# GpSimd adds each scan state's contribution to y_acc, and VectorE writes state times C to a buffer of its own

## The chip, the cores and the metric

The kernel runs on one core of one Trainium2 chip. The metric is the device time of one execution in microseconds. Of the five engines, TensorE does the matmuls and transposes, VectorE (DVE in the rows) and ScalarE (ACT) the elementwise work, SyncE (SP) issues all DMAs, and GpSimd (POOL) has no part in the kernel before. Each engine runs its own list of instructions in order, and they meet through semaphores.

## The reference, cut to what matters

x is 1024 tokens (16 sequences of 64) by 512. Three blocks follow each other, each with a residual.

```
x = x + cross_attention(layernorm(x), ctx)          # 8 heads, 512 keys for each sequence
n = layernorm(x)                                    # selective scan:
u = silu(conv4(n @ Wx) + cb)                        # 1024 channels, 4 taps
delta = softplus(n @ Wdt + b);  B, C = n @ Wb, n @ Wc   # 16 states
for t in time, for s in 16 states:
    h[s] = exp(delta * A[s]) * h[s] + delta * u * B[s]
    y   += C[s] * h[s]                              # starts from D * u
x = x + y @ Wout
x = x + sum over the top 4 of 16 experts (gate, up, down) of layernorm(x)
```

The line that matters is the one with C[s]: y is a sum over 16 states.

## The kernel before, in words

The tokens are cut into G = 4 groups of 256 (four sequences). A tile of one group's 1024 channels is 128 partitions x 2048 (8 blocks of channels by 256 tokens), f32. A state of the scan is four operations of VectorE over such tiles, in `scan_step`: part 0 writes u times B to `state` (L1074), part 1 runs the recurrence over time in place (L1077, `tensor_tensor_scan` with `decay`), part 2 multiplies `state` by C in place (L1080), part 3 adds it into `y_acc` (L1084). ScalarE makes `decay` for two states ahead (`scan_decay`, L855; two buffers), SyncE loads the broadcast rows of B and C (`load_bc`, L361; two buffers `bc_bcast`). ScalarE starts `y_acc` with D times u (`y_start`, L841), and TensorE reads the finished `y_acc` in the output projection (`out_proj`, L602, for the last group L674), after `step_done` has counted all states of the group.

The order on each engine is written out by hand. Groups overlap: while group g scans, the attention of group g + 1 runs. For VectorE the group loop reads: states 0 to 3 (LEAD = 4, with `key_bias`, L1017, after state 1), then 8 attention units with one state each, the unit's `neg_max` (L1023) between parts 0 and 1 and its `invert_sums` (L1065) between parts 1 and 2; then states 12 and 13 (TAIL = 2), `add_tiles` (L1031, the attention's result into `x_tokens`), the norm, and the signal `x1_rdy` on which SyncE loads the projection weights. States 14 and 15 follow while TensorE projects, then the convolution (`conv`, L1043), `scan_inputs`, and state 0 of the next group. In the next group's first state part 3 stands after `add_tiles` of the group before it.

The last group's states 1 to 15 run beside the experts: 64 jobs, in each of which TensorE does gate and up (`split_matmul`, L634) and down (L665). Jobs 4 to 42 hold the 60 parts of these states, one or two in each job (`scan_parts`). Beside them VectorE subtracts the high half of a weight to get the low half (`split_lo`, L1161), multiplies the gated pair (`hidden`, L1167 and L1168, PSUM inputs) and adds an expert's output into `x_tokens` (`add_expert`, L1179, PSUM input).

The convolution reads `conv_in`, whose three pad columns in front of each sequence VectorE zeroes once at the start (L1196).

Of the kernel before, what the change touches and what calls it, by code (L numbers as in the profile page):

```python
# [20 lines left out]
ALU = mybir.AluOpType  # L21
# [8 lines left out]
T = 64  # L30
# [4 lines left out]
G = 4  # L35
# [94 lines left out]
def perceiver_block(nc, x, ctx_t, ctx_n, wq_t, wk, wv_t, xp_t, dt_t, bc_t, ow_t, gate_t,  # L130
                    eg_t, eu_t, ed_t, params, bc_dram, out):
    with ExitStack() as es:
# [3 lines left out]
        def sem(name):  # L136
            return es.enter_context(nc.semaphore(name))
# [8 lines left out]
        comb_ = sb("comb", G * NT * E)  # L146
# [6 lines left out]
        hs_ = sb("state", SW)  # L153
        acc_ = sb("y_acc", SW)
# [10 lines left out]
        lgs = [sb(f"route_logits_{c}", NT * E)[:, :] for c in range(G)]  # L165
        sc, sfc, gs = (sb(f"route_{n}", NT * E)[:, :] for n in ("score", "choice", "group"))
# [11 lines left out]
        with ExitStack() as early:  # L178
# [13 lines left out]
            xi_ = sb("conv_in", 2 * 2 * XP, stack=early)  # L192
            xi = [xi_[:, s * 2 * XP:(s + 1) * 2 * XP].rearrange("p (k t) -> p k t", t=T + TAPS - 1) for s in range(2)]
# [37 lines left out]
        rank_ = sb("rank_scratch", 2 * NT * E * E)  # L231
        rk1, rk2 = (rank_[:, k * NT * E * E:(k + 1) * NT * E * E] for k in range(2))
# [58 lines left out]
        scan_rd = sem("decay_read")  # L291
        step_done = sem("scan_step_done")
# [38 lines left out]
        def _(sp):  # L331
# [24 lines left out]
            def load_bc(k):  # L356

                if k >= 2:
                    sp.wait_ge(step_done, k - 1)
                src = bc_dram[k // NS].rearrange("(w s) t -> s w t", w=2)[k % NS]  # L360
                sp.dma_start(bcs[k % 2], src.unsqueeze(0).to_broadcast([P, 2, GT])).then_inc(bc_in[k % 2], 16)  # L361
# [344 lines left out]
        def _(act):  # L706
# [98 lines left out]
            def proj_x(g, k0):  # L805
                n = g * NBK // 2 + k0 // 2
                b = job_a()
                act.wait_ge(pad_rdy, 1)
# [161 lines left out]

        @block.vector
        def _(dve):
# [60 lines left out]

            def conv(g, k0):
# [32 lines left out]
            def scan_step(g, j, parts=range(SCAN_PARTS)):  # L1067
# [11 lines left out]
                if 2 in parts:  # L1079
                    step(dve.tensor_tensor(h3, h3, cs, ALU.mult))  # L1080
                if 3 in parts:
                    if j == 0:
                        dve.wait_ge(ys_rdy, g + 1)
                    dve.tensor_tensor(acc_[:, :], acc_[:, :], h, ALU.add).then_inc(step_done, 1)  # L1084
                    dve.wait_ge(step_done, n + 1)
# [109 lines left out]
            for s in range(2):  # L1195
                ins = dve.memset(xi[s][:, :, 0:TAPS - 1], 0.0)  # L1196
            ins.then_inc(pad_rdy, 1)
# [15 lines left out]
            add_tiles(0)  # L1213
            dve.nop().then_inc(x1_rdy, 1)
# [7 lines left out]
            for g in range(G - 1):  # L1222
# [14 lines left out]
                add_tiles(g + 1)  # L1237
                dve.nop().then_inc(x1_rdy, 1)
# [96 lines left out]
```

## Time and profile before

| | us |
|---|---|
| Three runs | 1514.64, 1515.77, 1516.62 |
| Median | 1515.77 |
| Profiled execution, span from first to last instruction | 1514.9 |
| TensorE busy | 1281.5 |
| VectorE busy | 1157.1 |
| ScalarE busy | 599.0 |
| GpSimd busy | 0.2 |

The profiled execution has no time of its own beside its span; the runs' median lies 0.9 us above the span. Busy time is the sum of an engine's instruction times. An engine that is busy most of the time in a stretch may set its length; the chain of work that ended last, followed back from the end, says which engine did. The slices below cut the span in 40 parts of 37.9 us; a digit is a busy share in tenths.

```profile
PE   6998578868859758858758898999999999998998
DVE 1201899998999998999998848979888888446554
ACT  4432754554655535745536611131313131022220
POOL 0000000000000000000000000000000000000000
```

### The profile page before, as it was taken

What the parts mean: (1) busy time and instruction counts of PE and PEld (TensorE: products, weight loads), DVE (VectorE), ACT (ScalarE), POOL (GpSimd) and SP (SyncE); (2) the same over time, 40 slices, a digit from 0 to 9 for tenths busy, and PEclk for the clock granted to TensorE, in tenths of its full rate; (3) what the DMA queues carried; (4) which work ended last, traced back from release to release, by engine and by line L of the source; (5) the groups of instructions that cost most, each with busy time, mean ns of one, the idle gap of its engine ahead of it and who ended that gap; (6) DMA issues with size and microseconds to landing.
All of it is one profiled execution on the core that took longest, in us unless ns stands there. A gap on an engine that the chain in (4) does not pass through costs nothing.

```text
span 1514.9 us, 16115 instructions
## 1 busy us (share of the span) xinstructions
PE 1281.5 (85%) x6400; PEld 965.9 (64%) x6400; DVE 1157.1 (76%) x1001; ACT 599.0 (40%) x1229; POOL 0.2 (0%) x4
## 2 busy tenths in 40 slices
PE   6998578868859758858758898999999999998998
PEld 4776446646536547536537586777777777676775
DVE  1201899998999998999998848979888888446554
ACT  4432754554655535745536611131313131022220
POOL 0000000000000000000000000000000000000000
PEclk9999878988978978979879789999999999999999
DMA  7333013324013324013314201222222312114553
GB/s 247 101 121 127 6 25 116 104 63 133 8 49 91 118 54 128 10 49 110 89 57 145 91 22 35 86 61 70 56 77 63 84 49 63 56 44 152 168 160 103
DMA packets 95930, 128.47 MB, mean 85 GB/s; under 512 B 4976, under 2 KB 70640, under 8 KB 95856
## 3 DMA queue, kind: packets, MB, share of 16 engines
q1 hardware_dynamic: 95856, 127.45, 27.9%
q8 instruction: 51, 0.84, 0.2%
q14 instruction: 23, 0.19, 0.0%
HBM read 125.21 MB, written 2.23 MB: 84 GB/s over the span
## 4 chain that ended last, share of the span: by engine, by line
DVE 55%; PE 31%; ACT 8%; issue 3%; DMA 2%; DVEq 0%; ACTq 0%; SPq 0%
DVE state L1077 16%; PE bank L634 11%; DVE y_acc L1084 8%; DVE state L1074 8%; DVE state L1080 7%; PE bank L591 6%; PE bank L665 6%; ACT decay L855 4%; DVE x_tokens L1179 3%; DVE w_lo L1161 2%; DMA queries_ctx<-in_dt_t 2%; PE bank L520 2%; PE bank L545 2%; DVE hidden L1168 2%; DVE hidden L1167 2%
## 5 line engine op out<-in xcount | busy, mean ns | idle before, releaser
L1077 DVE TENSOR_TENSOR_SCAN state<-decay,state 128x2048 f32<-128x2048 f32 x64 | 282.9, 4420 | 8.3 <-ACT decay L855 7.2
L665 PE MATMUL bank<-w_down,hidden 128*128 128x512 f32 x512 | 232.1, 596 | 5.2 <-DVE x_tokens L1179 5.2
L634 PE MATMUL bank<-x_hi,w_hi 128*128 128x256 f32 x1024 | 192.6, 312 | 12.2 <-DVE hidden L1168 7.5
L855 ACT ACTIVATE decay<-delta_odd,params 128x256 f32<-128x256 f32 x256 | 106.3, 498 | 197.7 <-DVE state L1077 186.8
L634 PEld LDWEIGHTS bank<-x_hi,w_hi 128*128 128x128 f32 x1024 | 150.3, 198 | 43.5 <-issue 30.4
L520 PE MATMUL bank<-ctx,queries_ctx 128*128 128x256 f32 x512 | 151.8, 449 | 22.2 <-ACT queries_ctx L748 22.2
L634 PE MATMUL bank<-x_hi,w_lo 128*128 128x256 f32 x1024 | 168.9, 288 | 0.0
L634 PE MATMUL bank<-x_lo,w_hi 128*128 128x256 f32 x1024 | 168.7, 288 | 0.0
L902 ACT ACTIVATE hidden<-bank 128x512 f32<-128x512 f32 x64 | 38.0, 594 | 327.6 <-PE bank L665 321.5
L665 PEld LDWEIGHTS bank<-w_down,hidden 128*128 128x128 f32 x512 | 93.3, 191 | 100.5 <-issue 94.2
L1084 DVE TENSOR_TENSOR y_acc<-y_acc,state 128x2048 f32<-128x2048 f32 x64 | 146.7, 2292 | 2.3
L1080 DVE TENSOR_TENSOR state<-state,bc_bcast 128x2048 f32<-128x2048 f32 x64 | 146.2, 2284 | 1.4
L1167 DVE SCALAR_TENSOR_TENSOR hidden<-hidden,bank 128x512 f32<-128x512 f32 x64 | 43.8, 685 | 135.0 <-ACT hidden L902 134.8
L634 PEld LDWEIGHTS bank<-x_hi,w_lo 128*128 128x128 f32 x1024 | 145.6, 198 | 0.0
L634 PEld LDWEIGHTS bank<-x_lo,w_hi 128*128 128x128 f32 x1024 | 145.6, 197 | 0.0
L545 PE MATMUL bank<-probs,ctx 128*128 128x256 f32 x512 | 132.7, 417 | 14.9 <-ACT probs L782 14.9
L520 PEld LDWEIGHTS bank<-ctx,queries_ctx 128*128 128x128 f32 x512 | 109.1, 224 | 53.5 <-ACT queries_ctx L748 23.8
L855 ACT ACTIVATE decay<-delta_even,params 128x256 f32<-128x256 f32 x256 | 107.0, 500 | 79.7 <-DVE state L1077 71.3
L545 PEld LDWEIGHTS bank<-probs,ctx 128*128 128x128 f32 x512 | 104.4, 209 | 40.6 <-ACT probs L782 17.1
L591 PE MATMUL bank<-normed_t,queries_ctx 128*128 128x256 f32 x512 | 112.3, 381 | 2.4 <-DMA queries_ctx<-in_dt_t 1.3
L591 PEld LDWEIGHTS bank<-normed_t,queries_ctx 128*128 128x128 f32 x512 | 96.8, 190 | 19.5 <-DMA queries_ctx<-in_dt_t 3.7
L1161 DVE TENSOR_TENSOR w_lo<-raw_w,w_hi 128x1024 fp32r<-128x1024 f32 x64 | 77.0, 1224 | 33.3 <-ACT w_hi L883 31.9
(128 smaller groups left out, 1328.1 us busy)
## 6 DMA issues: line engine op xcount, KB each, us to landing
ctx<-in_ctx_t SPq DMA_DIRECT2D x32, 512.0 KB, 6.3
ctx<-in_ctx_n SPq DMA_DIRECT2D x32, 512.0 KB, 3.5
bc_bcast<-bc_scratch SPq DMA_DIRECT2D x64, 256.0 KB, 5.1
raw_w<-in_eg_t SPq DMA_DIRECT2D x32, 512.0 KB, 4.3
raw_w<-in_eu_t SPq DMA_DIRECT2D x32, 512.0 KB, 4.0
w_down<-in_ed_t SPq DMA_DIRECT2D x32, 512.0 KB, 4.8
queries_ctx<-in_dt_t SPq DMA_DIRECT2D x4, 2048.0 KB, 10.0
queries_ctx<-in_xp_t SPq DMA_DIRECT2D x4, 2048.0 KB, 14.8
```

What stands on the lines that cost most here:

```text
L520: pe.matmul(o, QT[:, k, c, qb * P:(qb + 1) * P], ctxT[n % 2][:, c, :], start=(c == 0), stop=False)
L545: mm = pe.matmul(b[:, cc * Q:(cc + 1) * Q], ctxN[n % 2][:, j, c * P:(c + 1) * P], probT[n % 2][:, j, :], start=(j == 0), stop=(j == KC - 1))
L591: mm = pe.matmul(b[:, kk * GT:(kk + 1) * GT], w[:, c, (k + kk) * P:(k + kk + 1) * P], xT[:, c, :], start=(c == 0), stop=(c == DC - 1))
L634: mm = pe.matmul(o, w[a](k), x[b](k), start=(q == 0), stop=(q == len(terms) - 1))
L665: mm = pe.matmul(b[t][:, :], hid[j % 2][:, i * GT + t * P:i * GT + (t + 1) * P], w_dn[k % 2][:, i, :], start=(i == 0), stop=(i == IC - 1))
L855: ins = act.activation(dA[n % 2][:, k * GT:(k + 1) * GT], dlt[g % 2][:, k, :], ACT.Exp, scale=par[:, c:c + 1])
L1074: step(dve.tensor_tensor(h3, u[g % 2], bs, ALU.mult))
L1077: dve.tensor_tensor_scan(h, dA[n % 2], h, 0.0, ALU.mult, ALU.add).then_inc(scan_rd, 1)
L1080: step(dve.tensor_tensor(h3, h3, cs, ALU.mult))
L1084: dve.tensor_tensor(acc_[:, :], acc_[:, :], h, ALU.add).then_inc(step_done, 1)
L1161: dve.tensor_tensor(lo, raw[q % RAW], hi, ALU.subtract).then_inc(w_rdy, 1)
L1167: step(dve.scalar_tensor_tensor(out=o, in0=o, scalar=1.0, in1=b[0][:, :], op0=ALU.add, op1=ALU.mult))
```

## The change

Part 3 leaves VectorE. Part 2 no longer multiplies in place: it writes to a new tile `state_c` and counts it in `hc_rdy`. GpSimd runs a list of its own: for each of the 64 states it waits for `hc_rdy`, adds `state_c` into `y_acc` and counts `step_done`. There is one `state_c`, so part 2 of the next state waits for `step_done` of the last one. SyncE's load of the next B and C rows waits for `hc_rdy` where it waited for `step_done`. To make room for the 8 KB a partition of `state_c`, `conv_in` moves into the memory of `probs`, where the attention overwrites its pads, so VectorE zeroes them once per group (`conv_pads`), and the small tiles of the router move behind the buffers of the experts.

```diff
+        hc_ = sb("state_c", SW)
...
-            xi_ = sb("conv_in", 2 * 2 * XP, stack=early)
-            xi = [xi_[:, s * 2 * XP:(s + 1) * 2 * XP].rearrange("p (k t) -> p k t", t=T + TAPS - 1) for s in range(2)]
+            xi = [pp_[:, s * 2 * XP:(s + 1) * 2 * XP].rearrange("p (k t) -> p k t", t=T + TAPS - 1) for s in range(2)]
...
                 if k >= 2:
-                    sp.wait_ge(step_done, k - 1)
+                    sp.wait_ge(hc_rdy, k - 1)
...
-                act.wait_ge(pad_rdy, 1)
+                act.wait_ge(pad_rdy, g + 1)
...
+        @block.gpsimd
+        def _(pool):
+            for n in range(G * NS):
+                if n % NS == 0:
+                    pool.wait_ge(ys_rdy, n // NS + 1)
+                pool.wait_ge(hc_rdy, n + 1)
+                pool.tensor_tensor(acc_[:, :], acc_[:, :], hc_[:, :], ALU.add).then_inc(step_done, 1)
+                pool.wait_ge(step_done, n + 1)
...
+            def conv_pads():
+                for s in range(2):
+                    ins = dve.memset(xi[s][:, :, 0:TAPS - 1], 0.0)
+                ins.then_inc(pad_rdy, 1)
...
                 if 2 in parts:
-                    step(dve.tensor_tensor(h3, h3, cs, ALU.mult))
-                if 3 in parts:
-                    if j == 0:
-                        dve.wait_ge(ys_rdy, g + 1)
-                    dve.tensor_tensor(acc_[:, :], acc_[:, :], h, ALU.add).then_inc(step_done, 1)
-                    dve.wait_ge(step_done, n + 1)
+                    if n >= 1:
+                        dve.wait_ge(step_done, n)
+                    dve.tensor_tensor(hc_[:, :].rearrange("p (k t) -> p k t", k=NBK), h3, cs, ALU.mult).then_inc(hc_rdy, 1)
+                    dve.wait_ge(hc_rdy, n + 1)
...
-            for s in range(2):
-                ins = dve.memset(xi[s][:, :, 0:TAPS - 1], 0.0)
-            ins.then_inc(pad_rdy, 1)
...
             add_tiles(0)
+            conv_pads()
             dve.nop().then_inc(x1_rdy, 1)
...
                 add_tiles(g + 1)
+                conv_pads()
                 dve.nop().then_inc(x1_rdy, 1)
```

VectorE in an attention unit of the first group's scan, before; `state_c_ready` below is the semaphore `hc_rdy`, `scan_step_done` is `step_done`.

```order
L1074 TENSOR_TENSOR state<-u_even,bc_bcast 128x2048 [waits bc_in1,scan_step_done]
L1023 TENSOR_REDUCE neg_max<-bank 128x2 [waits scores_full,dve_step]
L1077 SCALAR_TENSOR_TENSOR state<-decay,state 128x2048 [waits decay_ready]
L1065 RECIPROCAL row_sum<-row_sum 128x2 [waits probs_exp,decay_read]
L1080 TENSOR_TENSOR state<-state,bc_bcast 128x2048
L1084 TENSOR_TENSOR y_acc<-y_acc,state 128x2048 [waits dve_step]
L1074 TENSOR_TENSOR state<-u_even,bc_bcast 128x2048 [waits bc_in0,scan_step_done]
```

The same unit on VectorE with the change.

```order
L1090 TENSOR_TENSOR state<-u_even,bc_bcast 128x2048 [waits bc_in1,state_c_ready]
L1034 TENSOR_REDUCE neg_max<-bank 128x2 [waits scores_full,dve_step]
L1093 SCALAR_TENSOR_TENSOR state<-decay,state 128x2048 [waits decay_ready]
L1081 RECIPROCAL row_sum<-row_sum 128x2 [waits probs_exp,decay_read]
L1098 TENSOR_TENSOR state_c<-state,bc_bcast 128x2048 [waits scan_step_done]
L1090 TENSOR_TENSOR state<-u_even,bc_bcast 128x2048 [waits bc_in0,state_c_ready]
```

The add is gone from the unit, and the product with C has a wait that it did not have.

VectorE where the last state before the projections (state 13) ends and the norm begins, before.

```order
L1084 TENSOR_TENSOR y_acc<-y_acc,state 128x2048 [waits dve_step]
L1031 TENSOR_TENSOR x_tokens<-x_tokens,bank 128x512 [waits bankD_full,scan_step_done]
L1031 TENSOR_TENSOR x_tokens<-x_tokens,bank 128x512 [waits bankD_full]
L989 BN_STATS stats<-x_tokens 128x6 [waits bankD_free]
L989 BN_STATS stats<-x_tokens 128x6 [waits dve_step]
```

The same place with the change.

```order
L1098 TENSOR_TENSOR state_c<-state,bc_bcast 128x2048 [waits scan_step_done,decay_read]
L1042 TENSOR_TENSOR x_tokens<-x_tokens,bank 128x512 [waits bankD_full,state_c_ready]
L1042 TENSOR_TENSOR x_tokens<-x_tokens,bank 128x512 [waits bankD_full]
L1047 MEMSET probs 128x8x3 [waits bankD_free]
L1047 MEMSET probs 128x8x3
L1000 BN_STATS stats<-x_tokens 128x6
```

Here the add is gone too, and the two pad memsets stand ahead of the norm.

GpSimd's list with the change, its start; before, it held four memsets and nothing else.

```order
L972 UNCONDITIONAL_BRANCH [waits barrier_Pool_Activation_PE_DVE_SP_gather]
L978 ISA
L978 TENSOR_TENSOR y_acc<-y_acc,state_c 128x2048 [waits state_c_ready,y_started]
L978 TENSOR_TENSOR y_acc<-y_acc,state_c 128x2048 [waits state_c_ready,scan_step_done] x15
L978 TENSOR_TENSOR y_acc<-y_acc,state_c 128x2048 [waits state_c_ready,y_started,scan_step_done]
```

All 64 adds stand there, each behind its own product with C and the add ahead of it.

## Rows read from the trace of the kernel before

**Rows 1.** The page, part 1: busy time, share of the span, instructions.

```profile
PE 1281.5 (85%) x6400; PEld 965.9 (64%) x6400; DVE 1157.1 (76%) x1001; ACT 599.0 (40%) x1229; POOL 0.2 (0%) x4
```

**Rows 2.** The page, part 4: the chain that ended last, by engine.

```profile
DVE 55%; PE 31%; ACT 8%; issue 3%; DMA 2%; DVEq 0%; ACTq 0%; SPq 0%
```

**Rows 3.** The view by stretches, all engines; the columns stand in its first line.

```profile
core 0: us, PE busy (x) PEld busy (x) DVE busy (x) ACT busy (x) POOL busy (x), PEclk, DMA share, GB/s
397.65:564.45 166.80, 121.87 (x503) 86.07 (x501) 164.74 (x75) 88.87 (x217) 0.00 (x0) 0.85 0.25 71
564.45:616.33 51.88, 43.78 (x170) 32.24 (x171) 45.04 (x48) 26.58 (x42) 0.00 (x0) 0.86 0.32 97
868.00:1240.00 372.00, 358.17 (x2141) 283.75 (x2140) 295.74 (x321) 91.44 (x175) 0.00 (x0) 0.98 0.21 59
948.00:1240.00 292.00, 286.77 (x1734) 225.90 (x1733) 245.15 (x193) 76.64 (x148) 0.00 (x0) 0.99 0.24 67
```

**Rows 4.** VectorE in order of time, one attention unit of group 1.

```profile
444.81 2.29 DVE L1074 TENSOR_TENSOR state<-u_odd,bc_bcast 128x2048 f32<-128x2048 f32 x1
...
447.13 0.69 DVE L1023 TENSOR_REDUCE neg_max<-bank 128x2 f32<-128x512 f32 x1
...
447.74 4.41 DVE L1077 TENSOR_TENSOR_SCAN state<-decay,state 128x2048 f32<-128x2048 f32 x1
...
452.27 2.27 DVE L1080 TENSOR_TENSOR state<-state,bc_bcast 128x2048 f32<-128x2048 f32 x1
...
454.58 2.29 DVE L1084 TENSOR_TENSOR y_acc<-y_acc,state 128x2048 f32<-128x2048 f32 x1
...
456.90 2.29 DVE L1074 TENSOR_TENSOR state<-u_odd,bc_bcast 128x2048 f32<-128x2048 f32 x1
```

**Rows 5.** Groups of VectorE; columns: shapes, count, busy us, mean ns, idle before.

```profile
L1077 DVE TENSOR_TENSOR_SCAN state<-decay,state 128x2048 f32<-128x2048 f32 x64 | 282.9, 4420 | 8.3 <-ACT decay L855 7.2
...
L1084 DVE TENSOR_TENSOR y_acc<-y_acc,state 128x2048 f32<-128x2048 f32 x64 | 146.7, 2292 | 2.3
...
L1161 DVE TENSOR_TENSOR w_lo<-raw_w,w_hi 128x1024 fp32r<-128x1024 f32 x64 | 77.0, 1224 | 33.3 <-ACT w_hi L883 31.9
...
L1017 DVE TENSOR_TENSOR normed<-bank,params 8x2048 f32<-8x2048 f32 x4 | 9.1, 2279 | 15.9 <-PE bank L489 15.8
...
L1031 DVE TENSOR_TENSOR x_tokens<-x_tokens,bank 128x512 f32<-128x512 f32 x14 | 9.0, 683 | 18.1 <-PE bank L574 17.9
...
L1196 DVE MEMSET conv_in<- 128x24 f32 x2 | 0.1, 78 | 0.0
```

**Rows 6.** The same view of GpSimd, one of its four groups.

```profile
L1324 POOL MEMSET const-float32-0.0<- 128x1 f32 x1 | 0.1, 99 | 0.2 <-issue 0.2
```

**Rows 7.** The chain in order of time (start us, us, what): decay, then scan.

```profile
394.24 3.31 ACT decay L855 x8
397.65 4.44 DVE state L1077
```

**Rows 8.** VectorE in order of time, where group 1 hands over to group 2.

```profile
570.22 2.29 DVE L1074 TENSOR_TENSOR state<-u_odd,bc_bcast 128x2048 f32<-128x2048 f32 x1
...
585.22 4.42 DVE L1077 TENSOR_TENSOR_SCAN state<-decay,state 128x2048 f32<-128x2048 f32 x1 [1.27 <-ACT decay L855]
...
595.10 2.71 DVE L1043 SCALAR_TENSOR_TENSOR u_even<-conv_in,params,u_even 128x256 f32<-128x256 f32 x6 [0.80 <-ACT u_even L815]
...
600.17 5.34 DVE L1043 SCALAR_TENSOR_TENSOR u_even<-conv_in,params,u_even 128x256 f32<-128x256 f32 x12 [2.35 <-ACT u_even L815]
```

**Rows 9.** The same chain, one job of the expert stage: gate and up, then down.

```profile
1251.12 5.75 PE bank L634 x48
1256.87 3.44 PE bank L665 x8
```

**Rows 10.** The same chain: where two attention units of the first group begin.

```profile
52.12 3.65 PE bank L545 x16
...
61.11 3.65 PE bank L545 x16
```

More of the change, by code:

```diff
@@ L145, in perceiver_block @@
         bcT = nrm_[0:2 * NS, 0:GT]
-        comb_ = sb("comb", G * NT * E)
         xT_ = sb("normed_t", DC * GT)
@@ L163, in perceiver_block @@
         ident = par[:, C_ID:C_ID + P]
-        lgs = [sb(f"route_logits_{c}", NT * E)[:, :] for c in range(G)]
-        sc, sfc, gs = (sb(f"route_{n}", NT * E)[:, :] for n in ("score", "choice", "group"))
         st_ = sb("stats", 6 * G * NT)
@@ L231, in perceiver_block @@
         rank_ = sb("rank_scratch", 2 * NT * E * E)
+        comb_ = sb("comb", G * NT * E)
+        lgs = [sb(f"route_logits_{c}", NT * E)[:, :] for c in range(G)]
+        sc, sfc, gs = (sb(f"route_{n}", NT * E)[:, :] for n in ("score", "choice", "group"))
         rk1, rk2 = (rank_[:, k * NT * E * E:(k + 1) * NT * E * E] for k in range(2))
@@ L291, in perceiver_block @@
         scan_rd = sem("decay_read")
+        hc_rdy = sem("state_c_ready")
         step_done = sem("scan_step_done")
```

## The prediction, made before the changed kernel had run

> **What bounds the kernel now.** I read the busy times first: VectorE works 1157.1 us of the span of 1514.9, TensorE 1281.5, GpSimd 0.2 [rows 1]. The chain that ended last gives VectorE 55% of the span and TensorE 31% [rows 2]. Which of the two it is changes by stage, so the stretches come next [rows 3]. While the 14 scan states of group 1 run beside the attention of group 2 (397.65 to 564.45), VectorE is busy 164.74 of 166.80 us: it alone sets that stretch. There are three such stretches, for groups 0, 1 and 2. Between them (564.45 to 616.33) the chain goes through norm, weight transfer, projections and convolution; VectorE is busy 45.04 of 51.88 us there and runs states 14 and 15 while it would wait. In the expert stage (868 to 1240) TensorE is busy 358.17 of 372 us. So the 16 states of group 3 hardly touch the end: only the three VectorE stretches count.
>
> One attention unit of such a stretch [rows 4]: product with B at 444.81, neg_max at 447.13, scan at 447.74, product with C at 452.27, the add into y_acc at 454.58, the next product at 456.90. A unit is 456.90 - 444.81 = 12.09 us, and the add's slot in it 456.90 - 454.58 = 2.32 us (2.29 busy).
>
> **What is removed.** 64 adds of 2.29 us on VectorE [rows 5]. In each of the three stretches 14 of them (states 0 to 13) stand on the path: 14 x 2.32 = 32.5 us, 97.4 us in all. Those of states 14 and 15 and of group 3 are cover, worth nothing.
>
> **What is added.** 64 adds on GpSimd over the same 128x2048 tiles. The trace of before has no such operation: GpSimd did four memsets. From below I bound it by VectorE's own add, 2.29 us, from above by the slowest row over two tiles of this size, the scan of 4.42 us [rows 5]. GpSimd's memset of one element a partition takes 99 ns [rows 6], VectorE's of 24 takes 78 [rows 5]; of the two ends that is nearer to the slow one, and I take 4.42. The Trainium skill (GPSIMD Engine Reference, section "Elementwise — side-by-side cycle accounting") measures 4497 ns for this add against 2293 ns on VectorE; the trace agrees with the second, and by the first the sum below would be some 3 us higher.
>
> At 4.42 us the add is far shorter than a state, so if the two engines ran freely beside each other GpSimd would always be done before VectorE's next product with C, which now waits for it (one state_c buffer). The question is whether they run freely. Every VectorE operation of a state reads two tiles of SBUF, and so does the add. I forecast that the engines take turns: while GpSimd adds, no VectorE instruction with two SBUF inputs runs, and one waits for the other to end. Operations that read PSUM or a single tile go on. No row of before can show this, GpSimd being idle; it is a judgement, and the first rival is its opposite. The Trainium skill states it (SBUF — State Buffer, section "Who interferes with whom"): the second VectorE port pair is GpSimd's only one and "it's an exclusive lock"; no run here shows it yet. By that rule the change loses, without it it wins.
>
> **The sum with turns.** VectorE starts its next product about 0.03 us after the last (447.13 - 447.10 [rows 4]), and GpSimd, as an engine that is released by another, some 0.10 us after its releaser: the decay row ends at 394.24 + 3.31 = 397.55 and the scan that waited starts at 397.65 [rows 7]. So VectorE gets the next product with B in first, GpSimd takes its turn when that ends, and the scan follows. An add then costs 4.42 + 0.10 + 0.10 - 0.03 = 4.59 us of turn and returns 2.32: net 2.27 us, less what may run beside it. Per stretch:
> - Adds of states 3 to 10 fall beside a neg_max, which reads PSUM and takes 447.74 - 447.13 = 0.61 us of the path [rows 4]: 8 x (2.27 - 0.61) = 13.3 us.
> - Adds of states 2, 11 and 12 have nothing beside them: 3 x 2.27 = 6.8 us.
> - The add of state 1 falls beside the key-bias product from PSUM (2.28 us, the L1017 row [rows 5]): 0.
> - The add of state 0 falls beside two x_tokens adds from PSUM (2 x 0.68 = 1.3 us less overlap, the L1031 row [rows 5]): 1.0 us. Group 0 has no such adds, so 1.3 us more, once.
> - The add of state 13 falls beside x_tokens and the norm, which read PSUM or a single tile from 564.45 until the product at 570.22 [rows 8], over 4.6 us: the 2.3 us come off whole.
> That is 13.3 + 6.8 + 0 + 1.0 - 2.3 = 18.8 us; three stretches and the 1.3 make 57.7 us.
>
> States 14 and 15: the scan of 15 waited 1.27 us for its decay, the first convolution 0.80 us, the next ones 2.35 us [rows 8]. Two turns of 2.27 us go into these 4.4 us. I take 0; without that cover 4.5 us per hand-over.
>
> Expert stage: from 948 to 1240 VectorE is busy 245.15 of 292 us [rows 3], 47 us idle. A job of TensorE takes 5.75 + 3.44 = 9.19 us [rows 9], and 15 states are spread over 39 jobs, so a state has 39 x 9.19 / 15 = 23.9 us; 292 us hold 12.2 of them, with 3.9 us idle in each, and between a product with C and the next product with B a full set of PSUM-reading hidden and x_tokens operations always stands. Even bare, 2.27 us a state fits into 3.9. But an add that is under way blocks the w_lo subtraction (1.22 us, two SBUF inputs [rows 5]), and hidden and the down matmul queue behind that. I take 3 us for such moments, between 0 and 15 x 2.27 = 34.
>
> The pads: two memsets of 78 ns [rows 5] move from the start to each group, ahead of the signal that starts the weight load: 4 x 0.16, less 0.16 at the start, 0.5 us. ScalarE's wait for them is met long before, since norm, weight transfer and the first projections stand between. The B and C load on the sync queue now waits for the product with C, one add sooner than before, so it is never later. Where conv_in, comb and the logits lie in memory costs nothing, since attention of the group is over when conv_in is written.
>
> What queues behind the new waits: behind the product with C stands the whole VectorE queue, and through neg_max ScalarE's exponentials and TensorE's next scores; behind GpSimd's last add of a group stands only the output projection, which TensorE reaches only after the next group's projections.
>
> Sum: 57.7 + 0.5 + 3 = 61.2 us on the profiled span of 1514.9: 1576.1. The runs' median of 1515.77 lies 0.9 above that span; with it 1577 us.
>
> **The rivals.**
> 1. *The engines run freely (faster).* The 97.4 us come off, 0.5 us go on: 1515.8 - 96.9 = 1419 us. Would TensorE take over? A unit falls to 12.09 - 2.32 = 9.77 us, and the first group's attention, with no scan beside it, has units of 61.11 - 52.12 = 8.99 us [rows 10], so no. This decides if GpSimd's reads do not stop VectorE's. For it: no row shows a conflict. Against it: all it needs is the same tiles' memory at the same time.
> 2. *Turns, with no cover at all, or GpSimd served late.* If GpSimd's turn stops PSUM-reading work too, all 14 adds of a stretch cost 2.27: 3 x 31.8 = 95.3, with 0.5 and some 8 us in the expert stage 1620 us. If GpSimd only comes in after the scan, the neg_max cover alone is lost, 24 x 0.61 = 15 us: 1592.
> 3. *Turns, and the add as short as VectorE's.* 2.29 + 0.17 = 2.46 us a turn, 0.14 net. Per stretch 8 x (0.14 - 0.61) + 3 x 0.14 - 2.1 - 1.1 - 2.3 = -8.9; with the once-only 1.3 and 0.5 us, 1515.8 - 26.8 + 1.8 = 1491 us, faster. The point from which turns lose is an add of about 3.3 us. Against it: GpSimd's memset, slower than VectorE's.
> 4. *GpSimd falls behind its turn or its trigger, so that the wait for state_c does more than move the add.* It would need more than 9 us an add; I count it with rival 2.
>
> **Chances.** Forecast (turns, PSUM work beside them) 0.52, own range 1550 to 1600. Rival 2 0.26, rival 1 0.16, rival 3 0.04, and 0.02 for costs that cancel. What a measurement of this kernel can tell from no change is 0.2%, 3 us. Faster 0.20, same 0.02, slower 0.78. The range runs from 1486, a little under rival 3, to 1630, above rival 2, and leaves out the 0.16 of rival 1 and a little beyond the top.
>
> **What the changed profile would show.** Right: GpSimd adds end to start with VectorE's two-input operations; the unit's pitch near 12.09 + 1.66 = 13.75 us; an idle time of some 4 us in front of the scan in each unit while neg_max runs on time; expert stage as long as before; the stretch 397.65 to 564.45 longer by some 19 us. Wrong: a pitch of 9.8 us with GpSimd busy beside the scan (rival 1), neg_max late as well (rival 2), GpSimd adds starting well under 4 us apart in turn (rival 3), or a time under 1486.

## The result, and the profile after

| | before | after |
|---|---|---|
| Runs beside each other | 4 | 4 |
| Median, us | 1515.82 | 1550.29 |
| Lowest and highest, us | 1514.64 to 1516.62 | 1549.63 to 1552.22 |
| Span of the profiled execution, us | 1514.9 | 1548.9 |

The ratio after to before is 1.023, with an interval of 1.0215 to 1.0244: slower by 34 us. The forecast was 1577, slower by 61, with a range of 1486 to 1630; the result lies in the range, 27 us under the forecast and at the lower edge of the forecast's own 1550 to 1600. The page of after, part 1 and the head of part 4, to be read beside [rows 1] and [rows 2]:

```profile
PE 1287.7 (83%) x6400; PEld 968.2 (63%) x6400; DVE 1184.3 (76%) x943; ACT 596.7 (39%) x1229; POOL 372.4 (24%) x68
...
PE 48%; DVE 45%; ACT 5%; issue 2%; DMA 0%; DVEq 0%; SPq 0%; ACTq 0%
```

VectorE lost 64 adds of 2.29 us (146.7 us, [rows 5]) and its busy time rose all the same, from 1157.1 to 1184.3 us. GpSimd is busy 372.4 us. So something made VectorE's other operations longer. The groups of after, VectorE's and GpSimd's, say which (shapes, count, busy us, mean ns, idle before):

```profile
L1093 DVE TENSOR_TENSOR_SCAN state<-decay,state 128x2048 f32<-128x2048 f32 x64 | 414.1, 6470 | 15.3 <-ACT decay L856 14.1
L1098 DVE TENSOR_TENSOR state_c<-state,bc_bcast 128x2048 f32<-128x2048 f32 x64 | 146.2, 2284 | 1.4
...
L1090 DVE TENSOR_TENSOR state<-u_odd,bc_bcast 128x2048 f32<-128x2048 f32 x32 | 90.0, 2812 | 1.2
L1175 DVE TENSOR_TENSOR w_lo<-raw_w,w_hi 128x1024 fp32r<-128x1024 f32 x64 | 86.3, 1369 | 33.1 <-ACT w_hi L884 31.6
...
L1012 DVE TENSOR_SCALAR normed<-x_tokens,mean_var,rstd 128x512 f32<-128x512 f32 x16 | 10.0, 663 | 0.3
L1028 DVE TENSOR_TENSOR normed<-bank,params 8x2048 f32<-8x2048 f32 x4 | 9.1, 2279 | 15.5 <-PE bank L490 15.4
```

```profile
L978 POOL TENSOR_TENSOR y_acc<-y_acc,state_c 128x2048 f32<-128x2048 f32 x64 | 372.2, 5815 | 958.2 <-DVE state_c L1098 958.2
```

The scan's mean went from 4420 ns [rows 5] to 6470, w_lo's from 1224 to 1369; the product with C, which waits until GpSimd is done, kept its 2284, and the key-bias product from PSUM its 2279. In order of time the mechanism can be seen. VectorE and GpSimd in group 1 of after, around the adds of states 1 and 2 (433.52 and 447.12) and in one attention unit (from 473.67) (start us, us, engine, line), the counterpart of [rows 4]:

```profile
433.41 2.28 DVE L1028 TENSOR_TENSOR normed<-bank,params 8x2048 f32<-8x2048 f32 x1
435.83 4.35 DVE L1090 TENSOR_TENSOR state<-u_odd,bc_bcast 128x2048 f32<-128x2048 f32 x1
...
449.33 8.61 DVE L1093 TENSOR_TENSOR_SCAN state<-decay,state 128x2048 f32<-128x2048 f32 x1
...
473.67 2.29 DVE L1090 TENSOR_TENSOR state<-u_odd,bc_bcast 128x2048 f32<-128x2048 f32 x1
475.99 0.69 DVE L1034 TENSOR_REDUCE neg_max<-bank 128x2 f32<-128x512 f32 x1
476.60 8.00 DVE L1093 TENSOR_TENSOR_SCAN state<-decay,state 128x2048 f32<-128x2048 f32 x1
...
487.02 2.29 DVE L1090 TENSOR_TENSOR state<-u_odd,bc_bcast 128x2048 f32<-128x2048 f32 x1
```

```profile
433.52 4.52 POOL L978 TENSOR_TENSOR y_acc<-y_acc,state_c 128x2048 f32<-128x2048 f32 x1 [9.08 <-DVE state_c L1098]
447.12 6.54 POOL L978 TENSOR_TENSOR y_acc<-y_acc,state_c 128x2048 f32<-128x2048 f32 x1 [9.08 <-DVE state_c L1098]
...
473.78 6.54 POOL L978 TENSOR_TENSOR y_acc<-y_acc,state_c 128x2048 f32<-128x2048 f32 x1 [6.82 <-DVE state_c L1098]
```

One attention unit goes from the product with B at 473.67 to the next at 487.02: 13.35 us, where it was 12.09. GpSimd's row begins at 473.78, 0.11 us after VectorE's next product with B. That product takes its usual 2.29 us and ends at 475.96, neg_max from PSUM takes its usual 0.69, and the scan, which should take 4.42, takes 8.00. GpSimd's row ends at 480.32; 480.19 plus the scan's own 4.41 is where the scan ends. So the scan did its work only after the add (its last 0.13 us apart), and its waiting is inside its own duration: no idle time stands ahead of it. GpSimd's 6.54 us hold its own wait too: where it starts beside a PSUM product (433.52, key-bias) its row is 4.52 long. Beside the add of state 1 the next product with B takes 4.35 us for 2.29, and beside that of state 2, where nothing from PSUM stands, the scan 8.61 for 4.42. The two engines take turns, and each one's waiting for the other is printed as work.

The landmarks of both traces (each stretch is from the scan of state 0 to the first x_tokens addition behind state 13, each hand-over from there to the next group's scan of state 0), in us:

| | before | after | difference | forecast |
|---|---|---|---|---|
| start to the scan of state 0 of group 0 | 176.68 | 176.09 | -0.6 | |
| three stretches | 165.48, 166.80, 167.14 | 180.48, 180.82, 180.82 | +42.7 | +57.7 |
| three hand-overs | 55.49, 55.28, 63.59 | 56.42, 55.56, 66.05 | +3.7 | +0.5 |
| from the last group's scan of state 0 to the end | 664.44 | 652.66 | -11.8 | +3 |
| sum | 1514.9 | 1548.9 | +34.0 | +61.2 |

The stretches in the view by engine, after (the columns as in [rows 3]). The first is group 1's: VectorE is busy 179.24 of 180.82 us, as full as before. The third covers as much of the expert stage as the 868 to 1240 of before.

```profile
412.99:593.81 180.82, 126.05 (x503) 89.57 (x501) 179.24 (x60) 88.18 (x217) 81.08 (x13) 0.83 0.24 66
593.81:649.37 55.56, 47.23 (x178) 33.85 (x179) 46.87 (x48) 29.96 (x50) 15.61 (x3) 0.86 0.29 91
914.00:1286.00 372.00, 363.04 (x2195) 288.27 (x2195) 294.45 (x317) 91.29 (x175) 65.48 (x13) 0.98 0.21 62
```

In the same 372 us TensorE now gets through 2195 matmuls where it got through 2141 [rows 3]. A job is 56 of them and 9.19 us [rows 9], so after the 372 us it is 54 / 56 x 9.19 = 8.9 us further on (from 17.5 us behind the scan of state 0 to the end both traces hold the same 3613). The expert stage gained, where I had expected a small loss.

### The profile page after: what moved, and what is told of

It reads as the page before. It is cut to its first block, busy times and chain, and to the rows that moved or that the text cites. A ratio compares the mean times of both kernels' runs of the same rounds, so it can differ in the third digit from the quotient of the medians.

```text
span 1548.9 us, 16223 instructions
## 1 busy us (share of the span) xinstructions
PE 1287.7 (83%) x6400; PEld 968.2 (63%) x6400; DVE 1184.3 (76%) x943; ACT 596.7 (39%) x1229; POOL 372.4 (24%) x68
## 4 chain that ended last, share of the span: by engine, by line
PE 48%; DVE 45%; ACT 5%; issue 2%; DMA 0%; DVEq 0%; SPq 0%; ACTq 0%
DVE state L1093 21%; PE bank L635 20%; PE bank L666 12%; DVE state L1090 7%; DVE state_c L1098 6%; PE bank L592 6%; PE bank L521 2%; PE bank L546 2%; ACT decay L856 1%; DVE neg_max L1034 1%; PE bank L603 1%; PE bank L584 1%; PE bank L675 1%; DVE x_tokens L1193 1%; DVE w_lo L1175 1%
## 5 line engine op out<-in xcount | busy, mean ns | idle before, releaser
L978 POOL TENSOR_TENSOR y_acc<-y_acc,state_c 128x2048 f32<-128x2048 f32 x64 | 372.2, 5815 | 958.2 <-DVE state_c L1098 958.2
L1093 DVE TENSOR_TENSOR_SCAN state<-decay,state 128x2048 f32<-128x2048 f32 x64 | 414.1, 6470 | 15.3 <-ACT decay L856 14.1
L666 PE MATMUL bank<-w_down,hidden 128*128 128x512 f32 x512 | 232.1, 596 | 5.0 <-DVE x_tokens L1193 5.0
L521 PE MATMUL bank<-ctx,queries_ctx 128*128 128x256 f32 x512 | 156.3, 459 | 23.1 <-ACT queries_ctx L749 23.1
L666 PEld LDWEIGHTS bank<-w_down,hidden 128*128 128x128 f32 x512 | 93.3, 191 | 100.4 <-issue 94.2
L521 PEld LDWEIGHTS bank<-ctx,queries_ctx 128*128 128x128 f32 x512 | 112.6, 231 | 55.9 <-ACT queries_ctx L749 24.8
L1098 DVE TENSOR_TENSOR state_c<-state,bc_bcast 128x2048 f32<-128x2048 f32 x64 | 146.2, 2284 | 1.4
L1175 DVE TENSOR_TENSOR w_lo<-raw_w,w_hi 128x1024 fp32r<-128x1024 f32 x64 | 86.3, 1369 | 33.1 <-ACT w_hi L884 31.6
L592 PEld LDWEIGHTS bank<-normed_t,queries_ctx 128*128 128x128 f32 x512 | 98.3, 194 | 18.8 <-DMA queries_ctx<-in_dt_t 2.4
## 6 DMA issues: line engine op xcount, KB each, us to landing
queries_ctx<-in_xp_t SPq DMA_DIRECT2D x4, 2048.0 KB, 14.8
```

What stands on the lines that cost most here:

```text
L521: pe.matmul(o, QT[:, k, c, qb * P:(qb + 1) * P], ctxT[n % 2][:, c, :], start=(c == 0), stop=False)
L592: mm = pe.matmul(b[:, kk * GT:(kk + 1) * GT], w[:, c, (k + kk) * P:(k + kk + 1) * P], xT[:, c, :], start=(c == 0), stop=(c == DC - 1))
L666: mm = pe.matmul(b[t][:, :], hid[j % 2][:, i * GT + t * P:i * GT + (t + 1) * P], w_dn[k % 2][:, i, :], start=(i == 0), stop=(i == IC - 1))
L978: pool.tensor_tensor(acc_[:, :], acc_[:, :], hc_[:, :], ALU.add).then_inc(step_done, 1)
L1093: dve.tensor_tensor_scan(h, dA[n % 2], h, 0.0, ALU.mult, ALU.add).then_inc(scan_rd, 1)
L1098: dve.tensor_tensor(hc_[:, :].rearrange("p (k t) -> p k t", k=NBK), h3, cs, ALU.mult).then_inc(hc_rdy, 1)
```

## The experiments

All kernels below start from the changed one. The theory: while a GpSimd instruction reads SBUF, VectorE operations with two SBUF inputs stand still, and only as long as it reads; what is lost is the length of that standstill, called the hold below, less what VectorE can do from PSUM meanwhile. The rivals: the loss comes from the new wait and the buffer (the structure, not the memory); GpSimd disturbs VectorE whatever it does, writes included; the hold has a fixed cost for each instruction.

### No add at all

The add is left out everywhere; everything else stays, VectorE counts `step_done` itself. y lacks all states' contributions.

```diff
-                pool.tensor_tensor(acc_[:, :], acc_[:, :], hc_[:, :], ALU.add).then_inc(step_done, 1)
+                    dve.nop().then_inc(step_done, 1)      # on VectorE, behind the product with C
```

> The add into y_acc is left out on every engine (y_acc keeps only D times u); GpSimd has no work, everything else is as in the changed kernel. Theory of turns: the whole loss comes from GpSimd's adds holding VectorE up, so without them the 3 x 14 slots of 2.32 us are simply gone (97 us) and the expert stage keeps its gain of about 12 us: 1405 to 1421 us, attention unit 9.8 us. Rival (another engine or the new pads and layout would hold the kernel back anyway): above 1430 us, with a unit well over 10 us.

Measured: 1419.82 us (one run, before on the same chip 1520.12). A unit is 9.88 us, the stretches 140.81, 136.28 and 136.14. It is 100 us under before, and the changed kernel is 34 us over: each compared with before beside it, GpSimd's adds cost some 135 us as against no add at all. The time is also the 1419 of the prediction's first rival, free running, but made up otherwise: that rival took 97.4 us off the stretches, where 86.2 came off, and 9.8 us more came off the last part (654.66 for 664.44), which it had left alone.

### GpSimd writes and reads nothing

A memset of `state_c` stands in place of the add, with the same waits. y again lacks all states.

```diff
-                pool.tensor_tensor(acc_[:, :], acc_[:, :], hc_[:, :], ALU.add).then_inc(step_done, 1)
+                pool.memset(hc_[:, :], 0.0).then_inc(step_done, 1)
```

> In place of the add GpSimd sets state_c to zero: it writes 128x2048 and reads nothing (the sum over states is left out). Theory of turns about reading: VectorE's scan stays at 4.42 us although GpSimd works beside it, and the time is within 3 us of the kernel without adds. Rival (any GpSimd instruction holds VectorE's two-input operations up): the scan is stretched by the part of the memset that it meets, and the time lies above by 3 x 11 times that.

Measured: 1412.48 us (one run). VectorE and GpSimd in a unit of group 1:

```profile
444.01 2.29 DVE L1090 TENSOR_TENSOR state<-u_odd,bc_bcast 128x2048 f32<-128x2048 f32 x1
446.34 0.69 DVE L1034 TENSOR_REDUCE neg_max<-bank 128x2 f32<-128x512 f32 x1
446.94 4.41 DVE L1093 TENSOR_TENSOR_SCAN state<-decay,state 128x2048 f32<-128x2048 f32 x1
```

```profile
444.10 1.81 POOL L978 MEMSET state_c<- 128x2048 f32 x1 [7.96 <-DVE state_c L1098]
```

GpSimd writes the whole tile in 1.81 us, wholly inside VectorE's product with B, and that product keeps its 2.29 us, the scan its 4.41. A unit is 9.77 us. The new wait and the way through GpSimd cost the unit nothing (9.77 is 12.09 less the add's slot of 2.32), and writing does not hold VectorE: the rival of any disturbance is out. The kernel is 7 us faster than the one without an add, more than the 3 us that I had allowed: there each state had a `nop` that takes 0.11 us of VectorE's path (9.88 against 9.77). The 42 of them in the stretches make 4.6 us; the stretches differ by 6.4, of which 4.0 lie in the first, so some 2 us I cannot place. The Trainium skill (SBUF — State Buffer, section "Who interferes with whom") says just this, that a VectorE instruction with two SBUF inputs contends with a GpSimd instruction that reads SBUF and not with one that only writes.

### GpSimd reads one tile

A copy of `state_c` to `y_acc` in place of the add: one tile read, the same one written. y holds the last state alone.

```diff
+                pool.tensor_copy(acc_[:, :], hc_[:, :]).then_inc(step_done, 1)
```

> In place of the add GpSimd copies state_c over y_acc: one tile read instead of two (the sum over states is left out). Turns held for the length of any reading instruction: the scan is stretched by a hold of 1.7 to 2.4 us, and the time is 1465 to 1515 us. Rival (only an instruction with two SBUF inputs on GpSimd conflicts): scan at 4.42 us, the time that of the kernel without adds. Second rival (reads of the two engines share the rate instead of taking turns): the product with B that GpSimd's copy meets first is stretched too, over 2.29 us.

Measured: 1451.68 us (one run), a unit of 10.74 us. VectorE's scan and GpSimd's row:

```profile
453.05 2.29 DVE L1090 TENSOR_TENSOR state<-u_odd,bc_bcast 128x2048 f32<-128x2048 f32 x1
455.38 0.69 DVE L1034 TENSOR_REDUCE neg_max<-bank 128x2 f32<-128x512 f32 x1
455.98 5.39 DVE L1093 TENSOR_TENSOR_SCAN state<-decay,state 128x2048 f32<-128x2048 f32 x1
```

```profile
453.15 3.95 POOL L978 COPY y_acc<-state_c 128x2048 f32<-128x2048 f32 x1 [6.79 <-DVE state_c L1098]
```

The scan takes 5.39 us, 0.97 more than its own, and with the 0.61 us of neg_max ahead of it the hold is 1.58 us. Both lie under what I had written, the hold by 0.1 us (from 1.7) and the time by 13 us (from 1465). The product with B keeps its 2.29 us, so the two engines' reads do not share the rate. One input is enough to take a turn; the turn is shorter.

### Half the columns

The add over the first 1024 of the 2048 columns. The rest of y lacks the states.

```diff
+                pool.tensor_tensor(acc_[:, 0:SW // 2], acc_[:, 0:SW // 2], hc_[:, 0:SW // 2], ALU.add).then_inc(step_done, 1)
```

> GpSimd adds only the first 1024 of the 2048 columns (the other half of the sum is left out). Theory: the hold goes with the columns, 4.2 us for 2048 becomes 2.1, scan in an attention unit 4.4 + 2.1 - 0.6 = 5.9 us, unit 11.3 us; three stretches about 13 us each under those of before, time about 1469 us (1460 to 1480). Rival (a large fixed cost for each turn): a hold of 3 us or more, time above 1485 us.

Measured: 1464.13 us (one run), a unit of 11.20 us, near the 11.3 expected.

```profile
460.41 5.84 DVE L1093 TENSOR_TENSOR_SCAN state<-decay,state 128x2048 f32<-128x2048 f32 x1
```

```profile
457.58 4.39 POOL L978 TENSOR_TENSOR y_acc<-y_acc,state_c 128x1024 f32<-128x1024 f32 x1 [6.81 <-DVE state_c L1098]
```

The hold is 5.84 - 4.41 + 0.61 = 2.04 us, against 8.00 - 4.41 + 0.61 = 4.20 for the full tile: (4.20 - 2.04) / 1024 = 2.1 ns a column. At that rate 2048 columns alone would be 4.32 us, so no fixed part comes on top. This put a version with short adds within reach: an add whose hold fits under neg_max would cost the stretch nothing.

### All adds back on VectorE, everything else as changed

The control for the second buffer, the moved `conv_in`, the pads in each group and the moved router tiles. GpSimd has no work. `ON_POOL` is the list of states whose add GpSimd does, here empty.

```diff
+                if 3 in parts and n not in ON_POOL:
...
+                    dve.tensor_tensor(acc_[:, :], acc_[:, :], hc_[:, :], ALU.add).then_inc(step_done, 1)
+                    dve.wait_ge(step_done, n + 1)
```

> The changed kernel with one thing undone: VectorE does all 64 adds itself, out of state_c, where part 3 stood; state_c, the pads once per group and the layout stay. Theory: the loss is GpSimd's alone, so this is the kernel before plus the pads: 1514 to 1519 us. Rival (part of the 34 us is the pads, the layout or the product into a buffer of its own): 1522 us or more.

Measured, timed in three rounds with the next two: 1510.69 us (1508.64 to 1511.37; before 1517.11), ratio 0.9959, interval 0.9944 to 0.9974. The stretches are those of before to 0.4 us (165.47, 166.79, 166.78). So the loss is GpSimd's alone. But the kernel is 6 us faster than before, where I had expected at most 3: 5.3 us of it lie behind the last group's scan of state 0 (659.18 against 664.44). There the granted clock differs. The first 40 us of that part, before and in this kernel (stretch, us, TensorE busy and its matmuls, granted clock, DMA share, GB/s):

```profile
850.00:890.00 40.00, 30.88 (x195) 0.74 0.31 99
```

```profile
850.00:890.00 40.00, 31.73 (x203) 0.83 0.30 99
```

TensorE has a granted clock of 0.74 in the one and 0.83 in the other, and does 195 and 203 matmuls. Its two levels are 1.2 and 2.4 GHz, so it was at the full one for longer. Why it came up sooner I cannot say. It need not be the layout: the kernel with state 13 as well (below) was profiled twice, and from 20 to 40 us behind the scan of state 0 its two executions differ in the same way.

```profile
864.41:884.41 20.00, 17.75 (x117) 0.91 0.10 27
```

```profile
865.41:885.41 20.00, 17.75 (x110) 0.79 0.10 27
```

The first has 652.79 us in its last part and the second 656.89, 4.1 us more, of one and the same kernel. Before has 0.77 in these 20 us and the control 0.91. So most of the 5.3 us goes with the clock, and whether the layout has a part in it is not shown.

### GpSimd adds only beside the experts

The 16 states of the last group go to GpSimd, the 48 others stay on VectorE.

```diff
+        ON_POOL = list(range((G - 1) * NS, G * NS))
...
-            for n in range(G * NS):
+            for n in ON_POOL:
```

> GpSimd does only the 16 adds of the last group (beside the experts), VectorE the 48 others out of state_c. Theory: in the expert stage TensorE sets the pace and waits for VectorE's hidden only where a y_acc add stands ahead of it, so moving those adds gives the 9 to 12 us that the last part gained: 1503 to 1509 us. Rival (the last part was shorter for another reason, for instance another phase of the engines at its start): 1513 us or more.

Measured: 1502.42 us (1501.16 to 1503.41), ratio 0.9906, interval 0.9891 to 0.9921, 8.3 us under the control and 0.6 under the expected range. 6.8 us of them lie in the last part (652.39 against 659.18), and both kernels have the granted clock of 0.91 from 20 to 40 us into it. How long TensorE waited for `hidden` there, in before and in this kernel (us in total, times, longest; after has 2.5 us in two times):

```profile
PE bank L634 <- DVE hidden L1168: 7.5, 5, 2.1
```

```profile
PE bank L635 <- DVE hidden L1192: 2.3, 2, 2.1
```

The control has 7.1 us in five times, like before; with GpSimd adding here it is twice and 2.3 us. These 4.8 us are the larger part of the 6.8; the rest is not placed. One of the five in before, TensorE and VectorE:

```profile
1117.58 0.74 PE L634 MATMUL bank<-x_hi,w_hi 128*128 128x256 f32 x4 [1.45 <-DVE hidden L1168]
```

```profile
1106.18 4.42 DVE L1077 TENSOR_TENSOR_SCAN state<-decay,state 128x2048 f32<-128x2048 f32 x1
1114.99 1.23 DVE L1161 TENSOR_TENSOR w_lo<-raw_w,w_hi 128x1024 fp32r<-128x1024 f32 x1 [4.39 <-ACT w_hi L883]
1116.13 0.68 DVE L1167 SCALAR_TENSOR_TENSOR hidden<-hidden,bank 128x512 f32<-128x512 f32 x1
1116.84 0.69 DVE L1168 TENSOR_TENSOR hidden<-hidden,bank 128x512 f32<-128x512 f32 x1
```

The scan frees ScalarE for the next decay, w_hi stands behind that, and w_lo waits 4.39 us for w_hi; hidden comes 1.45 us too late for the gate and up matmuls. In after the same chain, with the same 4.39 us, stands at 1155.50, and TensorE does not wait for it: the add that stood ahead in VectorE's list is gone, and the chain is in time. Against TensorE's down matmuls (L665, then L666) the product with B ahead of this scan starts 0.51 us late in before (1103.85 against 1103.34) and 1.31 us early in after (1144.36 against 1145.67). VectorE had idle time in this stage, but not at the place where TensorE needed it. GpSimd's holds are paid out of VectorE's idle time: in the 372 us of after 13 adds of 2.29 us are gone, VectorE's busy time is 1.3 us less, and TensorE is 54 matmuls ahead.

### With state 13 as well

GpSimd also adds state 13 of groups 0 to 2, the one with x_tokens and the norm behind it.

```diff
+        ON_POOL = [g * NS + 13 for g in range(G - 1)] + list(range((G - 1) * NS, G * NS))
```

> As the run with the last group's adds on GpSimd, and in addition the add of state 13 of groups 0 to 2, which falls beside x_tokens and the norm. Theory: each takes 2.32 us off VectorE's path and gives 0.6 to 0.7 back, where the turn stretches the norm's first tensor_scalar: 3 x 1.7 = 5 us under the run with the last group alone, 1497 to 1504 us. Rival (the turn also stretches the statistics, or the weight load behind them is not released sooner): no difference or a loss against it.

Measured: 1500.33 us (1498.69 to 1502.94), ratio 0.9898, interval 0.988 to 0.9915. Each stretch is 2.33 us shorter (163.14, 164.46, 164.47), as forecast, and the hand-overs grow by 3.3 us together (56.67, 55.28, 64.95 against 54.97, 55.04, 63.54), so that 7.0 us come down to 3.0 by the profiled spans and 2.1 by the medians, where I had expected 5; the intervals of the two kernels overlap. VectorE behind state 13, here in after:

```profile
593.81 1.28 DVE L1042 TENSOR_TENSOR x_tokens<-x_tokens,bank 128x512 f32<-128x512 f32 x2
...
595.25 1.42 DVE L1000 BATCH_NORM_STATS2 stats<-x_tokens 128x6 f32<-128x512 f32 x2
...
597.52 1.65 DVE L1012 TENSOR_SCALAR normed<-x_tokens,mean_var,rstd 128x512 f32<-128x512 f32 x2
599.21 1.00 DVE L1012 TENSOR_SCALAR normed<-x_tokens,mean_var_x,rstd_x 128x512 f32<-128x512 f32 x2
```

The x_tokens addition (PSUM) and the norm's statistics (1.42 us, as before) go on during GpSimd's add (593.92 to 598.43); the norm's tensor_scalar, with one SBUF tile, does not: 1.65 us for 1.00. Its group has a mean of 663 ns where it had 544. The Trainium skill (SBUF — State Buffer, section "Who interferes with whom") has tensor_scalar among the operations that can use both of VectorE's ports; this row agrees. I had let every single-tile operation go free. But it does not explain the 3.3 us: it is there in each of the three hand-overs, and the second one grew by only 0.24 us.

### Slices that fit under the cover

GpSimd takes 256 of the 2048 columns of states 3 to 10 and 896 of state 1, and VectorE the rest; GpSimd begins when VectorE's part is done (`rest_done`), so that its hold falls on neg_max and the key-bias product. y is complete.

```diff
+        PART = {g * NS + j: (256 if j > 1 else 896) for g in range(G - 1) for j in [1] + list(range(LEAD - 1, LEAD + NU - 1))}
...
+                if n in PART:
+                    parts_seen += 1
+                    pool.wait_ge(rest_done, parts_seen)
+                    c = PART[n]
...
+                pool.tensor_tensor(acc_[:, 0:c], acc_[:, 0:c], hc_[:, 0:c], ALU.add).then_inc(step_done, 1)
...
+                    ins = dve.tensor_tensor(acc_[:, c:SW], acc_[:, c:SW], hc_[:, c:SW], ALU.add)
+                    if c:
+                        ins.then_inc(rest_done, 1)
```

> As the run with the last group's adds and those of state 13 on GpSimd. In addition GpSimd takes the first 256 of the 2048 columns of the adds of states 3 to 10 of groups 0 to 2, and 896 of those of state 1; VectorE adds the other columns, and GpSimd starts when VectorE's part is done. Theory: a hold of 256 columns is some 0.5 us (4.2 and 2.04 us for 2048 and 1024) and fits beside the neg_max slot of 0.61 us, so the scan is not stretched, and the unit falls by 256 columns of VectorE, 0.27 us, to 11.8 us; 3 x (8 x 0.27 + 0.93) = 9 us under the run without slices. Rival (a turn has a fixed cost that half and full adds hid, or the two queues meet badly): scan stretched by 0.3 us or more, no gain.

Measured, in three rounds with the next two: 1485.78 us (1484.81 to 1489.44; before 1514.99), ratio 0.9802, interval 0.9785 to 0.9818. VectorE and GpSimd in a unit:

```profile
458.33 2.03 DVE L1117 TENSOR_TENSOR y_acc<-y_acc,state_c 128x1792 f32<-128x1792 f32 x1
460.27 2.29 DVE L1101 TENSOR_TENSOR state<-u_odd,bc_bcast 128x2048 f32<-128x2048 f32 x1
462.60 0.69 DVE L1045 TENSOR_REDUCE neg_max<-bank 128x2 f32<-128x512 f32 x1
463.20 4.41 DVE L1104 TENSOR_TENSOR_SCAN state<-decay,state 128x2048 f32<-128x2048 f32 x1
```

```profile
460.44 2.71 POOL L990 TENSOR_TENSOR y_acc<-y_acc,state_c 128x256 f32<-128x256 f32 x1 [9.01 <-DVE y_acc L1117]
```

The product with B ends at 462.56, GpSimd's row at 463.15, inside neg_max, and the scan keeps its 4.41 us. A unit is 11.70 us, 0.39 under the 12.09 of [rows 4]. 0.26 of these are the shorter add (2.29 to 2.03); the rest comes from VectorE no longer waiting for its own add: the next product starts 1.94 us after a partial add of 2.03, where a full one of 2.29 had a slot of 2.32. I had expected a gain of 9 us over the version with state 13. The stretches gave 12.5, and 27 slices with 0.12 us each from the dropped wait explain the 3 us more: they are no gain of GpSimd's, and a kernel with only that wait dropped was not run. The profiled spans differ by 14.9 us, and the 2.4 outside the stretches are within what one kernel's executions differ by there (4.1 us in the last part). The medians differ by 18.0; the profiled execution of the slices was the slowest of its four.

### Slices wider than the cover

512 columns for 256, nothing else.

> As the run with slices of 256 columns, with 512 in the attention units. Theory: VectorE's add is 0.53 us shorter, but the hold of 1.0 us is 0.4 longer than the neg_max slot, so the scan lasts 4.8 us and the unit is 11.9 to 12.0 us: 3 x 8 x 0.15 = 3 to 4 us slower than slices of 256. Rival (no turns at this length, the two engines' reads share the rate): the unit falls to 11.6 us and the kernel is faster than with 256.

Measured: 1489.65 us (1487.32 to 1490.72), ratio 0.9827, interval 0.9813 to 0.9842; a unit of 11.78 us.

```profile
458.25 1.76 DVE L1117 TENSOR_TENSOR y_acc<-y_acc,state_c 128x1536 f32<-128x1536 f32 x1
...
462.86 4.76 DVE L1104 TENSOR_TENSOR_SCAN state<-decay,state 128x2048 f32<-128x2048 f32 x1
```

```profile
460.09 3.25 POOL L990 TENSOR_TENSOR y_acc<-y_acc,state_c 128x512 f32<-128x512 f32 x1 [8.54 <-DVE y_acc L1117]
```

The scan is stretched to 4.76 us, the hold is 0.35 + 0.61 = 0.96. VectorE's add is 0.27 us shorter than with 256 columns, and the scan 0.35 longer: 0.08 a unit the other way, as the units show. I had expected 0.15 (a unit of 11.9 to 12.0). That is 8 x 3 x 0.08 = 2 us, which the stretches show (481.5 against 479.5 in all). The medians differ by 3.9, with intervals that just overlap, while the profiled spans stand the other way round (1485.2 against 1487.4), by what lies outside the stretches. So the stretched scan and the direction in the stretches are as expected; that the whole kernel is slower than with 256 columns is not clear of noise.

### The version with state 13 once more

The same kernel as two headings above, on the chip of the sliced ones.

> The run with the last group's adds and those of state 13 on GpSimd, once more, beside the two with slices: 1497 to 1503 us, the base for both. Theory: both runs with slices lie below it, by 9 and by 5 to 6 us. Rival: neither does.

Measured: 1503.76 us (1503.22 to 1504.85), ratio 0.9923, interval 0.9908 to 0.9938, where it had 0.9898 the first time. The intervals just overlap, but it is 11.2 us under before here and was 16.8 under it there. It is the measure for the slices, which lie 18.0 and 14.1 us under it where I had expected 9 and 5 to 6, and a warning: 5 us between kernels that were not timed beside each other say nothing.

## Why the prediction was right or wrong

**That the engines take turns** was right. The write-only kernel shows it from the other side, and the first rival (free running, 1419) came near what it would be worth, 1412 to 1420 us where GpSimd does not read, though in part by luck: it had 97.4 us from the stretches and none from the expert stage, where 86.2 to 92.5 and 9.8 to 11.1 were measured.

**What goes on during an add.** Right for neg_max, x_tokens, the statistics and the key-bias product; wrong for tensor_scalar of the norm (0.65 us each time).

**The sum over a stretch** gave 18.8 us where 14.0 were measured in group 1. The step that failed is "an add costs 4.42 + 0.10 + 0.10 - 0.03 = 4.59 us of turn". The turn is 4.20. GpSimd's row alone is 4.52, 0.10 over my 4.42, but it does not hold VectorE for its whole length. In the unit above VectorE's product ends at 475.96, the scan works from 480.19, and GpSimd's row ends at 480.32. So some 0.16 us of its 4.52 pass while the product still runs and the last 0.13 while the scan already works; the gaps of 0.10 before and behind are not there, since the scan has long been issued and waits inside. With 4.20 - 2.32 = 1.88 for 2.27:

| | forecast | measured |
|---|---|---|
| a bare add (states 2, 11, 12) | +2.27 | +1.86 |
| beside neg_max (states 3 to 10), each | +1.66 | +1.26 |
| state 0 | +1.0 | +0.89 |
| state 1 | 0 | -0.26 |
| state 13 | -2.3 | -2.32 |
| stretch of group 1 | +18.8 | 3 x 1.86 + 8 x 1.26 + 0.89 - 0.26 - 2.32 = +14.0 |

The three stretches came to +42.7 for +57.7, 15.0 of the 27 us by which the forecast was too high. The eleven adds of states 2 to 12 at 0.4 us each make 13.3 of these. The bounds did not hold for the add itself: its row of 4.52 is above my upper bound of 4.42. That the value taken was near is luck, since the reason for the upper end was a memset of one element, and a memset of the whole tile takes GpSimd only 1.81 us.

**Hand-overs.** I took 0.5 us, with states 14 and 15 at nothing. Measured +3.7, of it 2.5 in the last one (63.59 to 66.05). The tensor_scalar rows account for at most 0.65 each. The second hand-over grew by 0.28 us, far under the 4.5 without cover, so states 14 and 15 cost nothing there, as forecast. The rest of the last one I have not taken apart; the kernel with state 13 as well had 64.95 and 66.75 us there in its two profiles.

**Expert stage.** I took +3 us. Measured -11.8, the largest miss beside the stretches. The failed step is "those of states 14 and 15 and of group 3 are cover, worth nothing": 7.5 us of TensorE's waits for hidden stood in the trace of before, in a view that the prediction did not read, and the kernel with GpSimd only in this stage waits 4.8 us less for hidden and gains 6.8 us. The 3 us for blocked w_lo did not come either: w_lo is 9.3 us longer in all (77.0 to 86.3), nearly all out of VectorE's idle time. The other 5.3 us are there without GpSimd (the control). Most of them goes with the granted clock, and why it differs stays open. Of the 27 us by which the forecast was too high, 15.0 come from the stretches, 14.8 from this stage and 0.6 from the start, less 3.2 from the hand-overs: two misses of one sign, and not one that covers the other.

**The form of the evidence.** I had written that an idle time of 4 us would stand ahead of the scan. There is none; it is in the scan's own duration. The unit's pitch was to be 13.75 and is 13.35; the stretch +19 and is +14.0. A reader who looked for idle time would have seen VectorE at 99% and taken the scan to have become slower in itself.

**The rivals.** Turns without cover (1620) and GpSimd served late (1592) are out by the timeline: neg_max is on time and GpSimd's add runs before the scan. A short add (1491) is out: the full one holds VectorE for 4.20 us. The point from which turns lose, given as 3.3, comes out nearer 2.9 from the prediction's own terms (between 1491 at 2.29 us and 1574 at 4.42, before the 3 us for the expert stage), and 4.20 is above either. GpSimd holds VectorE 2.1 ns for a column that VectorE adds in about 1.05. Only under cover it pays, and 0.61 us of cover is worth at least 0.61 / 2.1 ns = 290 columns, an estimate: 256 stretched no scan, 512 stretched it by 0.35 us and gave 0.08 a unit back.

## What to carry to other kernels

Work handed from VectorE to GpSimd is paid by VectorE at the length of the hold wherever its own operations have two SBUF inputs and GpSimd reads SBUF, here 2.1 ns a column for 1.05 saved; it gains only as far as VectorE has PSUM work or idle time right behind, and a slice cut to that cover (1485.78 us, 2.0% under before) beat both all and nothing. An engine with a low busy share can still be late at the few places where the bounding engine waits for it, so read the bounding engine's waits before an edit in its stage is put at nothing. To see a turn in a profile look for durations that have grown, not for idle time.

## What the runs showed of the hardware

- The hold of VectorE's two-input operations, worked out from the scan's extra time and neg_max's 0.61 us: full add 4.20 us, half 2.04, 512 columns 0.96, 256 columns no more than 0.61, copy of a full tile 1.58, memset of a full tile none. Of operations that read one SBUF tile, the norm's tensor_scalar was held (1.65 us for 1.00) and its statistics were not (1.42 both ways).
- A GpSimd add over 128x2048 f32 takes 4.50 to 4.54 us where nothing delays it and 6.54 where it must let VectorE's product end first; a memset of the same size 1.81 us.
- A `nop` of VectorE that counts a semaphore took 0.11 us of the path in each state.
- TensorE's granted clock in the same 40 us of the program was 0.74 or 0.83 for kernels that differ only in buffers, the pads and in where small tiles lie (195 and 203 matmuls, 5.3 us in the last part). One and the same kernel had 0.91 and 0.79 in two executions on two chips, with 4.1 us between them. No run here settles why.
